# A down product cut in two around the value projection, and the closing LayerNorm of the last rows on VectorE

## The reference

```python
def attn(h):                       # 16 heads of 32, 64 latent keys, top 4
    Q = (h @ Wq.T + bq)            # per head
    V = (h @ Wv.T + bv)            # per head
    logits = einsum('bhtd,lhd->bhtl', Q, latent) / sqrt(32)
    top, idx = top_k(logits, 4)
    w = softmax(top)
    weighted = sum_k w[k] * latent[idx[k]]
    return (weighted + V) @ Wo.T + bo

def ffn(h):                        # weights rounded to three values
    return (silu(h @ Wu.T) * (h @ Wg.T)) @ Wd.T      # 512 -> 2048 -> 512

x = x + layernorm(attn(layernorm(x)))
x = x + layernorm(ffn(layernorm(x)))
```

## Time and profile before

| | |
|---|---|
| median of 3 runs | 1047.22 us (1045.82 to 1048.94) |
| the profiled execution | 1049.91 us, of which 1048.1 us from first to last instruction |
| PE busy | 969.4 us, 92% |
| DVE busy | 736.0 us, 70% |
| ACT busy | 515.4 us, 49% |
| POOL busy | 542.8 us, 52% |
| stage "last" on PE | down(0) starts at 905.73, last down matmuls end near 955.3 |
| stage "tail" on PE | 955.13 to about 1040.5 |
| behind the last matmul | 1040.50 to the end at 1048.1 |

### The profile page before, as it was taken

How to read it: one execution, slowest core, us unless ns; L and a number is a source line. 1 busy time by engine, 2 the same in 40 slices (tenths; PEclk the granted TensorE clock), 3 DMA queues, 4 the chain that set the end, 5 groups by cost and what they waited for, 6 DMA issues and landing times.

```text
span 1048.1 us, 17870 instructions
## 1 busy us (share of the span) xinstructions
PE 969.4 (92%) x5738; PEld 472.0 (45%) x5738; DVE 736.0 (70%) x2668; ACT 515.4 (49%) x803; POOL 542.8 (52%) x448
## 2 busy tenths in 40 slices
PE   2474998899999999999999999999999999989997
PEld 1331544345444454445444454445444454435443
DVE  6997889746993769836994768836894768835331
ACT  4867887245454355345444455345453445323321
POOL 2466346664565446554565446654566445633332
PEclk9786999999999999999999999999999999999999
DMA  8944502434115321243023321253023311212001
GB/s 252 395 101 91 162 1 61 113 89 101 19 23 102 71 71 20 50 110 91 13 38 89 76 76 20 40 119 92 11 40 72 88 31 21 41 41 62 1 0 41
DMA packets 149335, 76.94 MB, mean 73 GB/s; under 512 B 135825, under 2 KB 135825, under 8 KB 148113
## 3 DMA queue, kind: packets, MB, share of 16 engines
q1 hardware_dynamic: 149264, 76.18, 29.1%
HBM read 34.21 MB, written 8.39 MB: 41 GB/s over the span
## 4 chain that ended last, share of the span: by engine, by line
PE 76%; DVE 10%; issue 4%; ACT 4%; DMA 3%; POOL 2%; SPq 0%; POOLq 0%; DVEq 0%; ACTq 0%
PE ug L668 36%; PE ug L685 17%; PE ring L534 12%; PE ring L646 6%; PE ring L582 2%; DVE Lr L1484 2%; DMA PT<-halves 1%; PE ug L534 1%; PE ring L626 1%; DVE v L1462 1%; DVE ugt L1447 1%; ACT TU L844 1%; DMA x_in<-in_x 1%; DVE halves L1442 1%; ACT TG L844 0%
## 5 line engine op out<-in xcount | busy, mean ns | idle before, releaser
L1183 POOL TENSOR_TENSOR hT<-ugt,hT 128x512 f16<-128x512 f32 x128 | 168.0, 1312 | 164.2 <-ACT hT L953 164.2
L668 PE MATMUL ug<-X1T,TU 128*128 128x512 f16 (+1 forms) x1152 | 245.1, 356 | 7.2 <-DVE ugt L1452 6.3
L668 PE MATMUL ug<-X1T,TG 128*128 128x512 f16 (+1 forms) x1152 | 244.8, 355 | 0.0
L685 PE MATMUL ug<-TD,hT 128*128 128x512 f16 x960 | 213.6, 383 | 3.2 <-issue 3.2
L946 ACT ACTIVATE ugt<-ug,cu 128x512 f32<-128x512 f32 x128 | 87.9, 687 | 204.0 <-PE ug L668 203.2
L668 PEld LDWEIGHTS ug<-X1T,TU 128*128 128x128 f16 x1152 | 110.5, 98 | 116.1 <-DVE ugt L1452 5.5
L668 PEld LDWEIGHTS ug<-X1T,TG 128*128 128x128 f16 x1152 | 112.7, 98 | 108.6
L1447 DVE SCALAR_TENSOR_TENSOR ugt<-ugt,ug 128x512 f32<-128x512 f32 x128 | 87.3, 682 | 100.3 <-ACT ugt L946 99.4
L685 PEld LDWEIGHTS ug<-TD,hT 128*128 128x128 f16 x960 | 94.0, 99 | 120.6 <-issue 11.0
L1484 DVE MATCH_REPLACE8 Lr<-v,Lb 128x68 f32<-128x68 f32 x512 | 102.4, 213 | 0.2 <-issue 0.2
L1517 DVE BATCH_NORM_STATS2 stf<-ug 128x6 f32<-128x512 f32 x30 | 20.8, 694 | 109.3 <-PE ug L685 109.3
(11 more groups left out here) (193 smaller groups left out, 1464.8 us busy)
## 6 DMA issues: line engine op xcount, KB each, us to landing
out_dram<-Lr SPq DMA_DIRECT2D x32, 256.0 KB, 3.1
x_in<-in_x SPq DMA_DIRECT2D x7, 1024.0 KB, 5.5
x<-in_x SPq DMA_DIRECT2D x28, 256.0 KB, 3.3
PT<-in_Wd SPq DMA_DIRECT2D x8, 512.0 KB, 8.1
hT<-in_Wu SPq DMA_DIRECT2D x4, 512.0 KB, 9.4
hT<-in_Wg SPq DMA_DIRECT2D x4, 512.0 KB, 15.1
x_in<-in_Wd SPq DMA_DIRECT2D x4, 512.0 KB, 5.2
x_in<-in_x SPq DMA_DIRECT2D x4, 256.0 KB, 4.2
```

The lines of the kernel that those rows point to most:

```text
L668: last = pe.matmul(ug[:, 2 * (e % 2) + s, cols], w[:, k, e * P:(e + 1) * P], X1T[:, b, k, cols], start=(k == 0 and b == 0), stop=(k == KD ...
L685: last = pe.matmul(down_bank(kind, t), hT[:, a, e, t * P:(t + 1) * P], td[:, e, :], start=(e == 0 and a == 0), stop=(e == NE - 1 and a == 1))
L1183: pool.tensor_tensor(hT[:, 1, e, :], ugt[:, 2 + e % 2, :], hT[:, 0, e, :], ALU.subtract).then_inc(h_lo, 1)
```

## The change

In the stage "last" only, down(1) is cut into two parts of 16 matmuls: the pieces 0 to 7 go right behind down(0), ahead of v(2), and the pieces 8 to 15 stay where down(1) was. `dn_done` is raised by the second part. The other stages keep their order.

```diff
-                def down(t):
+                def down(t, of=range(NE)):
...
-                    for e in range(NE):
+                    for e in of:
...
-                    last.then_inc(dn_done, 1)
+                    if NE - 1 in of:
+                        last.then_inc(dn_done, 1)
...
                     down(0)
-                    if nxt:
-                        down(1)
+                    down(1, range(NE if nxt else NE // 2))
                     v(2)
                     v(3)
                     weigh(0)
                     weigh(1)
-                    down(2 if nxt else 1)
+                    if nxt:
+                        down(2)
+                    else:
+                        down(1, range(NE // 2, NE))
```

```diff
+                def shift_residual(t):
+                    act.wait_ge(xn2_ready, TT * NCH)
+                    act.wait_ge(x1_lo, TT * NCH)
+                    act.activation(x_in[:, t, :], x_in[:, t, :], ACT.Identity, bias=nby_last[:, t:t + 1]).then_inc(res_shifted, 1)
...
                     if not att:
+                        if 4 <= e < 4 + TT:
+                            shift_residual(e - 4)
                         continue
...
+                if kind == "tail":                       (GpSimd)
+                    for t in range(TT):
+                        rstd_f(t)
+                    return
...
+                def f_centre(t):
+                    s = t % 2
+                    wait(dve, out_ready, j, TT, t - 1)
+                    wait(dve, out_stored[(t + 2) % 4], j, 16, 16 if t >= 2 else 0)
+                    dve.tensor_scalar(out_buf[s], down_bank(kind, t), mvf[:, s, 0:1], None, ALU.subtract).then_inc(f_bias, 1)
+
+                def f_close(t):
+                    s = t % 2
+                    wait(dve, f_rstd, j, TT, t + 1)
+                    dve.tensor_tensor(rcf[:, s:s + 1], rsf[:, s:s + 1], cf[:, 1:2], ALU.mult).then_inc(f_scale, 1)
+                    wait(dve, f_scale, j, TT, t + 1)
+                    wait(dve, f_bias, j, TT, t + 1)
+                    dve.wait_ge(res_shifted, t + 1)
+                    dve.scalar_tensor_tensor(out=out_buf[s], in0=out_buf[s], scalar=rcf[:, s:s + 1], in1=x_in[:, t, :],
+                                             op0=ALU.mult, op1=ALU.add).then_inc(out_ready, 1)
...
+                if kind == "tail":                       (VectorE)
+                    for t in range(TT):
+                        f_a(t)
+                        f_centre(t)
+                        f_close(t)
+                    return
```

More of the change, by code:

```diff
@@ L206, in build @@
         f_stats, f_mean, f_var, f_rstd, f_scale, f_bias, f_sum = (sem(f"f_{n}") for n in ("stats", "mean", "var", "rstd", "scale", "bias", "sum"))
-        out_ready = sem("out_ready")
+        out_ready, res_shifted = sem("out_ready"), sem("res_shifted")
         own_wait = sem("own_wait")
@@ L1083, in body @@
                     probs_hi(3)
-                if ffn:
+                if att and ffn:
                     f_rows(0)
@@ L1096, in body @@
                     f_rows(2)
-                else:
+                elif att:
                     f_rows(1)
@@ L1104, in body @@
                     t2_rows(0, 3)
-                if not nxt:
+                if kind == "last":
                     f_rows(2)
-                if ffn and not nxt:
                     f_rows(3)
@@ L1277, in body @@
                     probs_lo(3)
+                if kind == "tail":
+                    for t in range(TT):
+                        rstd_f(t)
+                    return
                 if ffn:
```

## The result

| | before | changed |
|---|---|---|
| median, 7 runs each | 1048.59 us (1045.82 to 1049.64) | 1042.87 us (1040.46 to 1043.43) |
| ratio | | 0.9946, 95% interval 0.9936 to 0.9956 |
| the profiled execution | 1049.91 us, span 1048.1 | 1042.87 us, span 1041.1 |

The account below looks back on a forecast made before the run. PE carries 76% of the 1048.1 us span, so only places where the chain leaves it can give time back. Gains of 4.2 (down product in halves) and 1.6 (kernel end) make 5.8: median 1047.22 becomes 1041.4, range 1039.6 to 1044.0.

Parts of the forecast that it names:

- The pause and its cover: PE ahead of the last chunk's weighing: 16 down(1) matmuls (3.45 us) fill the 3.17 us wait for the transposed probabilities.
- The low parts as the next bound: First output product: PE waits about 0.6 us for the fourth low part of the weighed values, leaving 4.2 of 4.8.
- the low clock: PE from 922.0 to 925.3, after the pause: clock at 0.50, costing 1.65 us, expected to stay at 1.00 after the change.
- Part A carried to the end: Second down product in halves, last chunk: its 4.2 us gain reaches the kernel's end through y_a(1) and PE's down matmuls.
- The order on GpSimd and VectorE: Before y_a(0): rstd_f(1) queues behind the fourth low part; the resulting 0.1 us delay vanishes in VectorE's 0.58 idle before y_a(1).
- Part B: Kernel end: VectorE subtracts the mean while GpSimd makes rstd, then closes the row; gain 1.6 us, or 1.2 with rstd at 1.00.
- The residual shifts: Four added ScalarE operations in the tail, 0.81 us each, free under the 2.25 us idle before each tanh; 3.3 us if uncovered.
- Rival 4: Tail on ScalarE: the shifts hold back the tanh; at 5.0 us each, 11 us longer, time 1052.4; chance 0.03.
- rival 1: PE behind the pause: the clock falls only in some executions; without it the sum is 4.1 us, time 1043.1; chance 0.15.
- Rival 2: Low parts of the weighed values and rstd: new waits take more; sum 4.6 us, time 1042.6; chance 0.08.
- Rival 3: Transposed probabilities land later in step with PE, so only 1.6 us is left, time 1045.6; chance 0.05.

Follow-up runs that it names:

- All-early: Changed kernel with all 32 matmuls of down(1) ahead of v(2) instead of 16; 0.9982 of the kernel before, 1.9 us under it.
- seven pieces: Changed kernel with 14 matmuls of down(1) ahead of v(2) instead of 16 and the constant factor folded into f_centre; 0.9950 of the kernel before, median 1043.05 us.
- filler kernel: Kernel before with 14 more matmuls, whose results nobody reads, between v(3) and the weighing; 0.9983 of the kernel before, 1.8 us faster.
- a quarter ahead: Changed kernel with 8 matmuls of down(1) ahead of v(2) instead of 16, and 24 behind the weighing; 1043.82 us in one execution.
- part B alone: Kernel before with only the tail's rows changed (VectorE centres and closes them, residual shifted beforehand), PE's order kept; 0.9982 of the kernel before, 1.9 us faster.

## Why the prediction was right

Forecast: 1041.4 us, a gain of 5.8 on the median of the three runs then shown; measured 5.7 and 1042.87. Of the 1.5 us between the times 1.4 is the reference: the median of the kernel before rose from 1047.22 over 3 runs to 1048.59 over 7. Point by point:

- **The pause and its cover.** Right. Of 3.17 us of pause 0.1 is left. The weighing started 15.63 us behind down(0), where 921.26 - 905.73 = 15.53 was predicted: the 0.1 is a gap between the last value matmul and the weighing that I had set to nothing.
- **The low parts as the next bound.** Right. The wait was predicted as 0.6 us and measured as 0.57. All-early and seven pieces show from both sides that this chain is the bound: started 3.46 us later (924.20 - 905.11 = 19.09 behind down(0)) it makes D1 longer by 3.78, of which 0.3 is the low clock that came there; started 0.38 earlier it makes it shorter by 0.38.
- **Part A carried to the end.** Right: 4.07 against 4.2. The 0.13 is the gap of 0.1 above, which delays the whole chain, and rounding. The tail's first up product starts 45.33 us behind down(0) and not 49.40, so all of it arrives there.
- **The order on GpSimd and VectorE.** rstd_f(1) did come behind the fourth low part, and y_a(0) started with no idle time before it. It was absorbed before y_a(1).
- **Part B.** Right: 1.62 against 1.6. f_centre took 0.74 instead of the 0.70 taken, at the upper of the two rows that bounded it; it still ended level with rstd, so the sum didn't move.
- **The residual shifts.** 0.71 us instead of 0.81, covered by idle time of which 1.64 is left. Rival 4 had nothing to stand on.
- **The step that was only half right: the low clock.** The prediction counted 1.65 us for it as if it came each time and gave rival 1 a chance of 0.15. The price is right (1.63 by the filler kernel), but in two of four traces of the old order there was no fall. Where it doesn't fall, the whole change is worth 2.4 + 1.6 = 4.0 us. The measured 5.7 (4.6 to 6.7) says that the fall is common in the timed runs, and leaves room for executions without it: with a fall in half of them it would be 4.9, inside the interval. So rival 1 is true of single executions. That the measured gain agrees to 0.1 with a forecast that counts a fall each time is partly luck; a chance of 0.15 was too low for what one trace could show.
- **Rival 2** fell: VectorE's statistics of down(1) ran from 925.11, during the second pair of low parts, and that pair took 2.40 as the first. **Rival 3** fell: the landing of PT isn't seen in the changed kernel, where PE no longer waits for it, but ScalarE's step ahead of it starts where it did (6.73 us behind down(0), 6.72 before), and with a quarter ahead, where PE waits again, the weighing starts at 15.25 as before.

## What to carry to other kernels

When an engine waits in the middle of a chain, look for independent work that can be cut, and put into the gap just as much as fills it: half of the down product was worth 4.1 us (2.4 where the clock doesn't fall), all of it about nothing (D1 30.3 against 30.6 with a fall and 29.0 without one; in the timed runs as fast as part B alone), since the rest is needed to cover the next link of the same chain. A gap that costs the clock costs more than its length, but a single trace doesn't tell how often; price the two apart and look at several executions. At the end of a kernel, compute what needs only the mean while another engine makes the variance's power, and, where that engine is GpSimd, give it a VectorE neighbour that doesn't read two SBUF tensors.

## What the runs showed of the hardware

- The fall of TensorE's clock from 2.4 to 1.2 GHz at a pause of 3.2 us came in two of four traces, with the pause equal to 0.02 us in all of them. It began 0.4 us before the end of the pause in one and 0.9 us behind it in the other, was as long in both, and cost 1.4 and 1.6 us. Behind 1.4 us (one trace) and behind the waits of 0.6 us in the changed order it didn't come; in the all-early order it came behind 2.1 us of waiting, three matmuls and another wait.
- A GpSimd power of 128x1 took 0.99 us beside a 128x512 VectorE operation with two SBUF inputs and 0.55 beside one that reads PSUM, in the same place of the program. It ended 0.4 us behind the end of its neighbour with two SBUF inputs.
- Subtracting a scalar from a PSUM bank of 128x512 on VectorE took 0.742 us; with a second scalar operand, which multiplies, 0.802.
